# Turning x on VectorE in a gated cross-attention and memory kernel: one core, three stages rearranged

## What is computed

```
x = x + tanh(g_xattn) * attention(layernorm(x), ctx)
    Q = ln(x) Wq^T + bq ; K = ctx Wk^T + bk ; attn = softmax(Q K^T / sqrt(2048)) ; attended = attn @ ctx
x = x + tanh(g_ffn) * ffn(layernorm(x))
    query = h Wq'^T (64) ; router scores over 512 slots ; top 8 ; softmax over them ; values of the slots
    aux = values @ Wvd^T @ Wvu^T
    u = clip(0.5 * log1p(var h)/mean + 2.5 * sigmoid(gelu(h Wu1^T + bu1) Wu2^T + bu2), 0, 5)
    out = h + gate(u) * aux
```

## Time and profile before

| | us |
|---|---|
| median of 3 runs (1189.83 to 1191.6) | 1190.06 |
| the profiled execution | 1191.12 |
| its span | 1189.3 |
| keys, from the span's start to | 139.4 |
| score weights | 139.4 to 255.9 |
| slot weights (`ffn_block`) | 256.3 to 303.1 |
| tokens | 303.1 to 1017 |
| output | 1017 to 1189.3 |

### The profile page before, as it was taken

One profiled execution on the slowest core, in us unless ns is written; L12 is line 12 of the kernel. 1 busy time (PEld: TensorE's weight loads), 2 busy tenths in 40 slices (PEclk: granted clock), 3 DMA queues, 4 the chain that ended last, 5 costly groups with the idle time before them and its releaser, 6 DMA issues. The chain is left out here.

```text
span 1189.3 us, 21180 instructions
## 1 busy us (share of the span) xinstructions
PE 1123.4 (94%) x7402; PEld 1070.5 (90%) x7402; DVE 745.3 (63%) x1888; ACT 453.3 (38%) x743; POOL 180.0 (15%) x275
## 2 busy tenths in 40 slices
PE   7999878899899999999999999999999996599998
PEld 6999878887899999999999999999999995488886
DVE  6555665456326676666667666767676755777776
ACT  4333323434213333433433343434333334444553
POOL 0000330000001212121212222121212121400000
PEclk9999989899899999999999999999999997799999
DMA  7333449787428712320112311113201025889999
GB/s 283 136 137 139 118 140 314 219 280 253 106 66 208 196 53 71 106 87 35 71 35 71 122 64 41 45 61 106 87 35 71 35 71 140 284 304 403 427 427 381
DMA packets 114647, 185.28 MB, mean 156 GB/s; under 512 B 45876, under 2 KB 95060, under 8 KB 97624
## 3 DMA queue, kind: packets, MB, share of 16 engines
q1 hardware_dynamic: 109432, 147.11, 37.8%
q10 hardware_dynamic: 4608, 33.56, 6.7%
q0 software_dynamic: 576, 4.19, 0.8%
HBM read 140.55 MB, written 54.79 MB: 164 GB/s over the span
## 5 line engine op out<-in xcount | busy, mean ns | idle before, releaser
L46 PE MATMUL tk_hidden_sum<-b_weights,k_turned 128*128 128x384 f32 x512 | 180.2, 352 | 0.0
L48 PE MATMUL tk_hidden_sum<-b_weights,k_turned 128*128 128x384 f32 x512 | 172.5, 337 | 0.0
L47 PE MATMUL tk_hidden_sum<-b_weights,k_turned 128*128 128x384 f32 x512 | 171.7, 335 | 0.0
L46 PE MATMUL tk_b_sum<-b_weights,k_turned 128*128 128x320 f32 (+1 forms) x528 | 166.5, 315 | 0.0
L48 PE MATMUL tk_b_sum<-b_weights,k_turned 128*128 128x320 f32 (+1 forms) x528 | 164.0, 311 | 0.0
L47 PE MATMUL tk_b_sum<-b_weights,k_turned 128*128 128x320 f32 (+1 forms) x528 | 163.5, 310 | 0.0
L963 ACT ACTIVATE k_turned<-tk_bank 128x512 fp32r<-128x512 f32 x128 | 76.4, 598 | 202.9 <-PE tk_bank L76 185.1
L1130 DVE TENSOR_TENSOR k_turned<-tk_bank,k_turned 128x512 fp32r<-128x512 f32 x128 | 88.3, 691 | 66.1 <-ACT k_turned L963 65.6
L46 PEld LDWEIGHTS tk_b_sum<-b_weights,k_turned 128*128 128x128 f32 x528 | 99.3, 188 | 0.3
L47 PEld LDWEIGHTS tk_b_sum<-b_weights,k_turned 128*128 128x128 f32 x528 | 99.3, 188 | 0.0
L48 PEld LDWEIGHTS tk_b_sum<-b_weights,k_turned 128*128 128x128 f32 x528 | 99.1, 188 | 0.0
(11 more groups left out here) (264 smaller groups left out, 2608.9 us busy)
## 6 DMA issues: line engine op xcount, KB each, us to landing
k_rows<-in_x_dram SPq DMA_DIRECT2D x54, 1024.0 KB, 4.9
out_dram<-k_rows ACTq DMA_DIRECT2D x22, 1024.0 KB, 10.6
k_rows<-in_Wk_dram SPq DMA_DIRECT2D x16, 1024.0 KB, 4.8
k_rows<-in_Wq_dram SPq DMA_DIRECT2D x16, 1024.0 KB, 6.0
ob_x<-in_x_dram SPq DMA_DIRECT2D x10, 1024.0 KB, 10.5
out_dram<-ob_x ACTq DMA_DIRECT2D x10, 1024.0 KB, 11.0
b_weights<-scratch_b SPq DMA_DIRECT2D x6, 1024.0 KB, 6.9
scratch_mt<-k_way_out SPq DMA_DIRECT2D x32, 128.0 KB, 2.5
```

The costliest lines, as they stand in the source:

```text
L46: pe.matmul(out, lh, rh, start=start, stop=False, skip_group_check=skip)
L47: pe.matmul(out, lh, rl, start=False, stop=False, skip_group_check=skip)
L48: return pe.matmul(out, ll, rh, start=False, stop=stop, skip_group_check=skip)
```

## The change

**VectorE turns x.** x is loaded as blocks (`load_blocks`): partition 32q + j holds the tokens 32k + j of quarter q of the columns, in four DMAs. VectorE transposes 32x32 blocks of it from SBUF into the bank, reading every sixteenth column. The result has column 16p + c of x in partition p of chunk c, so all the weights that meet x are laid out in the same way (`spread`): the transposes of the context, Wk, the feed-forward Wq and Wu1 take every sixteenth column, and so do the products of the score weights. TensorE makes no transposes of x.

**ScalarE takes the moments.** A second, plain copy of x (`load_rows`) gives the row sum (a Copy with a sum) and the sum of squares around the mean (a Square with a bias and a sum); POOL makes mean and variance from them. x is no longer centred. The rows of Wq, of the feed-forward Wq and of Wu1 are centred in its place, the last two by ScalarE in `ffn_block`. Each copy of x has one buffer (`rows[2]`, `rows[3]`); the small results move to `rows[0]` and `rows[1]`.

**Slot weights one tile later.** TensorE turns the slot weights of tile t-2 after the first quarter of b of tile t, and makes the values of t-2 after b. VectorE and ScalarE follow.

**Score weights over whole rows.** Step n takes 128 whole rows of Wq (all 2048 columns, in a ring of three buffers) and adds 16 x 3 products to 16 halves of eight banks, over all steps. The banks are emptied after the last one, and stored in eight DMAs; the stage after waits for them at job 4.

```diff
-def load_wq(sp, io, rows, sems, n, u):
...
+def load_wq(sp, io, keep, n):
+
+    sp.dma_start(keep["rows"][wq_slot(n)][:], io["Wq"][n * P:(n + 1) * P, :]).then_inc(keep["wq_in"][n % WQ_RING], 16)
...
+def wq_high(act, keep, n):
+
+    return act.activation(keep["T"][n % 2][0][:].rearrange("p c x -> p (c x)"), keep["rows"][wq_slot(n)][:],
+                          ACT.Identity, bias=keep["wq_nmean"][:, n:n + 1])
...
+            def step(n, u, first=False, last=False):
+                hi, lo = (spread(t[:].rearrange("p c x -> p (c x)")) for t in T[u])
+                if not first:
+                    pe.wait_ge(lo_done, n)
+                for c in range(KC):
+                    ins = split_product(pe, bank[c // 2][:, (c % 2) * CR:(c % 2 + 1) * CR],
+                                        (hi[:, c, :], lo[:, c, :]),
+                                        (at(KT[0], n), at(KT[1], n)), first and c % 2 == 0, last, True)
...
-        c = 4 * g + k
-        ins = pe.transpose(bank[:, k * rows:(k + 1) * rows], src[0:rows, c * P:(c + 1) * P],
-                           ident[0:rows, 0:rows])
+        c = 4 * g + k
+        part = slice(c, D, KC) if spread else slice(c * P, (c + 1) * P)
+        ins = pe.transpose(bank[:, k * rows:(k + 1) * rows], src[0:rows, part], ident[0:rows, 0:rows])
...
+            def centre(n):
+
+                own, r = rows[ffn_buffer(n)], jobs[n][0]
+                act.wait_ge(rows_in[ffn_buffer(n)], 16 * (n // FFN_RING + 1))
+                act.activation(own[0:r, :], own[0:r, :], ACT.Copy, accum_out=row_sum[0:r, :])
+                act.drain()
+                act.activation(row_nmean[0:r, :], row_sum[0:r, :], ACT.Copy, scale=-1.0 / D)
+                act.drain()
+                act.activation(own[0:r, :], own[0:r, :], ACT.Identity,
+                               bias=row_nmean[0:r, 0:1]).then_inc(centred, 1)
+
             for n, (r, dst) in enumerate(jobs):
+                if n + 1 in CENTRED_JOBS:
+                    centre(n + 1)
                 if n == WVU:
                     continue
+                if n == CENTRED_JOBS[0]:
+                    act.wait_ge(keep["mt_out"], MT_STORED)
...
+        def load_tile(sp, t):
+            sp.wait_ge(S["turned"], G * t)
+            load_blocks(sp, io, keep, t)
+            sp.wait_ge(S["squares"], t)
+            load_rows(sp, io, keep, t)
...
                 b_part(t, u, 0)
+                if late_z_too:
+                    late_turn_w(t - 2)
                 b_part(t, u, 1)
                 if late:
-                    late_query(t - 1, late_first)
+                    late_query(t - 1)
                 b_part(t, u, 2)
                 b_part(t, u, 3).then_inc(S["b_sum"], 1)
+                if late_z_too:
+                    late_z(t - 2)
                 if late:
-                    late_route(t - 1, late_first)
+                    late_route(t - 1)
                 a_part(t, u, 0, first)
-                if not last:
-                    pe.wait_ge(S["centred"], t + 2)
-                    turn_x(t + 1, 1 - u, 0)
                 a_part(t, u, 1, first)
-                if not last:
-                    turn_x(t + 1, 1 - u, 1)
...
+            def row_sum(t, u):
+                act.wait_ge(keep["plain_in"], 16 * t + 16)
+                act.activation(plain[:], plain[:], ACT.Copy, accum_out=rsum[u][:]).then_inc(S["row_sum"], 1)
...
+            def turn_x(t, g):
+                dve.transpose(bank[g % 2][:].rearrange("p (c k j) -> p c k j", c=4, j=LANES),
+                              blocks[:].rearrange("p (k i c) -> p c k i", k=P // LANES, c=KC)[:, 4 * g:4 * g + 4]
+                              ).then_inc(S["turned"], 1)
...
                 if late:
                     late_stats(t - 1, 1 - u, (j if u else j - 1) // 4, second)
                     late_scale(t - 1, 1 - u)
+                if not (last or first):
+                    turn_ready(t + 1)
+                    turn_x(t + 1, 0)
+                    turn_x(t + 1, 1)
+                if late:
                     late_q_lo(t - 1)
                     late_poly(t - 1)
+                if not (last or first):
+                    x_lo(t + 1, 1 - u, 0)
+                    x_lo(t + 1, 1 - u, 1)
                 soft_scores(t, u, j // 4)
...
+                elif not last:
+                    turn_x(t + 1, 2)
                 soft_att(t, u, first or second)
+                if late_z_too:
+                    late_z(t - 2)
...
+                if not last:
+                    turn_x(t + 1, 3)
                 if late:
                     late_slots(t - 1)
                 if not last:
-                    x_lo(t + 1, 1 - u, 0)
-                    x_lo(t + 1, 1 - u, 1)
+                    x_lo(t + 1, 1 - u, 2)
+                    x_lo(t + 1, 1 - u, 3)
                 att_lo(t)
                 if late:
                     late_learned(t - 1, 1 - u)
-                if ahead:
-                    moments_of(u, j + 1, (0, 1))
```

More of the change, by code:

```diff
@@ L16 @@
 QN = 512
+QUADS, LANES = 4, 32
+WQ_RING = 3
 GROUPS = KC // 4
@@ new lines, in _ @@
+            for b in range(KC // 2):
+                dve.wait_ge(out_hi, b + 1)
+                dve.tensor_tensor(out[1][:, 2 * b:2 * b + 2, :], bank[b][:].rearrange("p (c n) -> p c n", c=2),
+                                  f32(out[0][:, 2 * b:2 * b + 2, :]), ALU.subtract).then_inc(out_lo, 1)
+        @block.tensor
+        def _(pe):
+            def step(n, u, first=False, last=False):
[6 more added lines that the diff above has]
+                                        (at(KT[0], n), at(KT[1], n)), first and c % 2 == 0, last, True)
+                    if last and c % 2 == 1:
+                        ins.then_inc(product, 1)
+                if not last:
+                    ins.then_inc(used, 1)
+            step(0, 0, first=True)
+            step(1, 1)
+            with pe.Fori(1, KC // 2 - 1) as j:
@@ L444, in ffn_jobs @@
+            step(KC - 1, 1, last=True)
 def ffn_jobs(io):
@@ L871, in late_z, with tile @@
                 ins.then_inc(S["z_sum"], 1)
[L873 removed]
+            def tile(t, u, late=True, late_z_too=True, first=False, second=False, j=None):
                 pe.wait_ge(b_in, 32 * b_of(j) + 32)
@@ L1275, in gates, with tile @@
                 op(dve.tensor_scalar, keep["f_att"][:], keep["f_x"][:], tgx[:, 0:1], None, ALU.mult)
-            def tile(t, u, j, late=True, last=False, ahead=True, first=False, second=False):
+            def tile(t, u, j, late=True, late_z_too=True, last=False, first=False, second=False):
                 if late:
```

517 lines of the change are left out of this document (263 added, 254 removed).

## The result

| | before | after |
|---|---|---|
| median, us | 1189.94 (4 runs) | 1220.13 (4 runs) |
| span of the profiled execution, us | 1189.3 | 1219.5 |
| TensorE busy, us | 1123.4 | 1149.2 |
| VectorE busy, us | 745.3 | 766.0 |
| ScalarE busy, us | 453.3 | 559.2 |

The changed kernel is slower: 1.0254 times the time of before, 95% interval 1.0242 to 1.0267, that is 30 us more. 1152 was forecast, with a range of 1127 to 1190.

What follows compares the result with a forecast made beforehand. TensorE was taken to bound the token tiles, VectorE holding up the score weights' start. Terms -51.8 - 1.1 + 16 - 4 + 0.5 + 1.5 = -39 us, from 1191.1 to 1152 us; range 1127 to 1190.

Steps and rivals of the forecast that it cites:

- The strided load: Keys' transposes and score-weight products: loading stationary columns 64 bytes apart taken as 0; upper end 0.22 us spacing.
- rival (a): Keys' transposes and score-weight products: strided array loads cost, 0.10 to 0.11 x 1056 = 112 us, 1264 us; chance 0.15.
- The -4: Score weights over whole rows, including a longer keys' stage: -4 us, bounds -11 to +6.
- the better of the two cases: Score weights' start: first row's low part gets in between POOL's two operations, done at 11.4 us, otherwise 21.1.
- The walk of the tile: One token tile in the new order, timed from its first product: VectorE ends at 16.4 us, TensorE at 18.5.
- 51.8: Token tiles: TensorE without x's transposes takes 18.50 us against 20.17, a gain of 1.67 on 31 tiles.
- Nothing waits: Token stage's loads of x, one buffer per copy: arrive in time; counted 0, 0 to 10 us for the stage.
- The slot weights: Slot-weight stage: ScalarE centres rows for five jobs, 4.4 us each, partly covered; +16 us, bounds +8 to +20.
- The tail: After the last tile: tile 30's turn and values precede tile 31's routing on TensorE; +1.5 us (0 to 4).
- (b): Token tiles: VectorE's turns cost over 1.35 us and set the tile; 1183 us at 1.6 us a turn; chance 0.08.
- (c): Token tiles: the single block buffer is filled too late, 14 us instead of 10.6; 1257 us; chance 0.04.
- (d): Slot and score weights: centring mostly hidden, or POOL's grip on VectorE costs less; 1135 us; chance 0.05.

Runs made afterwards that it cites:

- pairs: Changed kernel with the parts of Wq laid out so two neighbouring columns of every sixteen stay together, products loading at 8 bytes; 1168.6 us, 0.982 of before.

## Why the prediction was wrong, point by point

**The strided load** is the step that failed. It was the sentence "I take 0, because no row shows TensorE paying for how an operand lies". The upper end named beside it, a spacing of 0.22 us, is what the trace shows to the digit. The row that it should have gone by was the strided one, from which VectorE's turn had been given an extra cycle a column; it was applied to one engine and not to the other. What is measured: 0.10 us on each of 768 products, 77 us that the sum had at 0, and next to nothing on 288 transposes, where rival (a) had both, 112 us. Rival (a) was the right mechanism with the right sign; its 1264 was 44 us too high. Of that, 29 us are the transposes (288 x 0.106 less 1 to 2 measured) and 4 the price of the products (0.106 against 0.10); for some 13 the slow products covered waits that the forecast had charged in full (the stage has 4 us beside its 16 x 10.66 of products, where the forecast had some 18). The other stages add up to 3 us the other way.

**The score weights otherwise.** The -4 can't be read from the changed kernel, since its slow products cover other waits, and no version has the stride's price gone with everything else as it was. With pairs the stage takes 121.9 us, 5 more than before, but there VectorE's low part is in eight pieces, which met POOL's work worse; with POOL's pieces in the keys, 108.5. In the changed kernel the low part of row block 1 did get in between POOL's two instructions, done at 155.7, which is 11.3 us in, as the better of the two cases had it:

```profile
144.50 9.04 POOL L389 TENSOR_TENSOR a_cent<-k_turned,k_mu_all 128x4096 f32<-128x4096 f32 x1 [143.01 <-POOLq L97]
...
150.24 5.45 DVE L350 SCALAR_TENSOR_TENSOR a_T<-k_rows,a_wq_nmean,a_T 128x2048 fp32r<-128x2048 f32 x1 [1.75 <-ACT a_T L343]
153.62 10.91 POOL L391 TENSOR_TENSOR a_cent<-a_cent,k_turned 128x4096 f32<-128x4096 f32 x1
```

What the walk left out is the low part of the next row block. It begins at 157.6, lasts until 166.7 beside POOL's second instruction, and lets step 2 start 22 us into the stage, not 17. The forecast also had 1.3 us for emptying the banks, where with fast products TensorE waits 5.4. An estimate from these rows, step 2 at 22.3 us, 14 steps of 5.76 and 5.4 us for the banks, gives 108 us. That is 9 less than before and, with the 5 us that the keys grew (2.9 forecast), near the -4 that was taken.

**The tiles.** 18.50 us was taken from the last tile of before, 18.52 was measured. The 20.17 that it was set against is a mean with tile 0 in it, which takes 17.96 us; most tiles take 20.24. The walk of the tile held: in the tile that starts at 952.59 VectorE's scores begin 7.96 us in (forecast 7.85), the fourth turn ends at 11.7 (11.1), the slots at 14.6 (14.2), and ScalarE's squares at 17.5 (17.5). The turn's cost did not: 1.07 us, not the 0.75 taken, within the bounds of 0.69 and 1.22. It cost nothing, since it stayed under the 1.35 at which it would.

What is missing from 51.8 are the places where the steady order does not hold. "Nothing waits" was said of the loads, and was wrong twice. First, tile 0, SP's queue, VectorE and TensorE in time:

```profile
430.94 0.43 SPq L860 DMA_DIRECT2D scratch_cw<-k_z  x1
431.42 3.35 SPq L724 DMA_DIRECT2D k_rows<-in_x_dram  x4
...
440.37 1.96 DVE L1197 STREAM_TRANSPOSE tk_bank<-k_rows 128x512 f32<-128x512 f32 x2 [7.53 <-DMA k_rows<-in_x_dram]
...
444.04 0.48 PE L963 MATMUL tk_small<-k_ident,k_rows 128*128 128x128 f32 x1 [7.57 <-DVE k_rows L1228]
```

Tile 0's last turn ends at 426.2, but its blocks are replaced only from 431.4 on, behind a store of the context weights for which SP waits; they land at 440.4. In tile 0 VectorE takes the turns of tile 1 ahead of the attention, and TensorE's attention transpose waits 7.57 us. With two buffers for x this queue position cost nothing. In the two versions with the load ahead of that store TensorE's wait is 1.0 and 2.8 us. Second, at each of the three changes of batch the next weights, 2 MB, share the queues with the four block loads, and a tile is longer by 1.2, 1.2 and 0.2 us (0 to 1.2 in the other versions):

```profile
581.15 0.41 PE L54 MATMUL tk_b_sum<-b_weights,k_turned 128*128 128x320 f32 x1 [1.00 <-DMA b_weights<-scratch_b]
```

From its first product to the next tile's, tile 0 takes 27.7 us instead of 18.0, and tile 1 17.7 instead of 20.2: together 7.3 us longer than before, where 3.3 less was forecast. The changes of batch add 2.5, and the 29 other tiles gain 1.72 us each instead of 1.67. Together that is about the 11.4 us by which the tiles missed. The steps of the walk were right, but it was a walk of one steady tile.

**The slot weights.** Right in mechanism and size: +14.4 against +16, 4.25 us a job against 4.4, and 16.1 us gone without the passes. Five times 4.25 is 21.3 us, so some 5 to 7 of it were hidden, as forecast.

**The small terms.** The tail (+1.4 against +1.5) and the context products (-2.7 against -1.1) are near. The output stage, charged 0, is 5.2 us shorter. It is 166 to 168 us in every kernel of this study that has the new token stage, and 171 in the two that have the old one. The traces show where: at the stage's start POOL makes passes over weights (128x2048, 4.6 us each), and VectorE scales what TensorE turns next. POOL, VectorE and TensorE in time, before and then after:

```profile
1030.11 9.23 POOL L696 TENSOR_TENSOR b_weights<-b_weights 128x2048 fp32r<-128x2048 f32 x2 [2.51 <-ACT b_weights L689]
1034.86 4.56 DVE L1466 TENSOR_SCALAR ob_att_z<-k_z,k_f_z 128x128 f32<-128x128 f32 x1
1039.48 0.48 PE L1392 MATMUL ob_turned<-k_ident,ob_att_z 128*128 128x128 f32 x1 [5.50 <-DVE ob_att_z L1466]
```

```profile
1069.80 0.28 DVE L1561 TENSOR_SCALAR ob_att_z<-k_z,k_f_z 128x128 f32<-128x128 f32 x1
1069.87 4.73 POOL L766 TENSOR_TENSOR b_weights<-b_weights 128x2048 fp32r<-128x2048 f32 x1 [0.20 <-ACT b_weights L759]
1070.13 0.33 PE L1487 MATMUL ob_turned<-k_ident,ob_att_z 128*128 128x128 f32 x1 [1.07 <-DVE ob_att_z L1561]
```

Before, VectorE's scaling of 0.28 us falls into POOL's last pass, lasts 4.56, and TensorE waits 5.50 us. After, it gets in just ahead of that pass, and TensorE waits 1.07. It is so in all 13 traces, 5.5 us in the two with the old stage and 1.1 in the others, which is 4.4 of the 5.2 us. The new order got this by luck: nothing in the change aims at it.

**Rivals (b), (c) and (d).** (b) and (c) did not happen in the steady tiles; (c), the single buffer filled too late, happened in tile 0 alone. (d) did not happen either: no more of the centring was hidden than the forecast had taken off.

## What to carry to other kernels

A layout that one engine gets for free is paid for by whoever reads it: before TensorE, ScalarE or VectorE reads an operand with a stride, ask whether each 16 bytes still give two float32 elements, and if not, try to keep pairs together, which here was worth 51 us (TensorE's transposes were the exception). Read the starts of products and not the busy share, for a stage at 98% busy had its products nearly twice as far apart as before. Walk the first tile and the batch changes as well as the steady one, above all when two buffers become one, and look for waits that slow work had covered: they appear when the work gets fast. Look at which of POOL's long passes VectorE's work meets, and cut them into pieces where TensorE waits behind it.

## What the runs showed of the hardware

- The load of a 128x128 stationary operand for the split products sets the pace at 0.23 us when its columns lie 16 bytes apart (0.24 at 32, 0.22 at 64), whether the moving operand has 256, 320 or 384 columns; at 4 and 8 bytes the product sets it (0.12 us at 256 columns). At 64 bytes the price is lowest, which a count of lines does not give. Nothing between 8 and 16 bytes was run.
- TensorE's float32 transposes, whose stationary operand lay 64 bytes apart too, kept almost their pace: four in 0.38 us instead of 0.35, with a load's record of 0.20 us instead of 0.14.
- ScalarE's pass of 2048 float32 columns takes 2.0 us dense, 2.1 in pairs of 8 bytes, 3.9 for single columns 64 bytes apart, and 3.9 when it writes single columns.
- VectorE's 32x32 turn of 128x512 float32 from SBUF to a bank takes 0.71 us dense and 1.07 with columns 64 bytes apart; its three-operand pass of 2048 columns goes from 2.35 to 3.8 us when one operand is read at 64 bytes.
- Beside POOL's passes of 4096 columns (9 to 11 us), VectorE passes that take 2.35, 3.8 and 0.47 us alone lasted 9.06, 11.4 and 9.03 us; beside one of 2048 columns (4.6 us), one of 0.28 us lasted 4.56. In pieces of 256 columns (0.76 us each) in the keys, POOL's work cost nothing that the stage's end shows (144.0 and 145.4 us, 146.0 without it).
